# The first cross attention of a two-layer decoder, rewritten as a stage that projects its own keys and values

## The reference, cut to what matters

```
q = x @ Wcq + bcq                 # (4, 256, 128), 16 heads of 8
k = ctx @ Wck + bck               # (4, 1601, 128)
v = ctx @ Wcv + bcv
a = softmax(q k^T / sqrt(8))      # per batch and head: 256 x 1601
o = a v                           # then added, through Wp, to x
```

## Time and profile before

| | |
|---|---|
| three runs | 2718.17, 2724.49, 2734.19 us |
| the profiled execution | 2717.35 us |
| its span | 2715.6 us |
| mean granted TensorE clock | 0.847 of full speed |
| PE busy | 2050.7 us (76%) |
| DVE busy | 1267.7 us (47%) |
| ACT busy | 955.5 us (35%) |
| POOL busy | 389.2 us (14%) |

### The profile page before, as it was taken

How to read it: one execution, slowest core, us unless ns; L and a number is a source line. 1 busy time by engine, 2 the same in 40 slices (tenths; PEclk the granted TensorE clock), 3 DMA queues, 4 the chain that set the end, 5 groups by cost and what they waited for, 6 DMA issues and landing times. The chain is left out here.

```text
span 2715.6 us, 46818 instructions
## 1 busy us (share of the span) xinstructions
PE 2050.7 (76%) x17125; PEld 1118.7 (41%) x17125; DVE 1267.7 (47%) x2794; ACT 955.5 (35%) x1300; POOL 389.2 (14%) x334
## 2 busy tenths in 40 slices
PE   2853396989886299677999336743999999999498
PEld 1532261323334155424666203431455555555365
DVE  2842387778882333351443324534444444442322
ACT  1521161656663222102332113412244444444133
POOL 2110211000000000091111123410111111110100
PEclk7975596888998599797999667976699999999699
DMA  5428723132220001123221165301111111110010
GB/s 175 106 72 226 214 61 75 49 74 66 67 61 1 24 35 35 55 101 112 58 58 39 53 187 135 91 24 46 42 35 36 44 44 44 44 41 2 1 41 29
DMA packets 266743, 183.18 MB, mean 67 GB/s; under 512 B 27924, under 2 KB 252380, under 8 KB 265948
## 3 DMA queue, kind: packets, MB, share of 16 engines
q1 hardware_dynamic: 266588, 181.05, 24.3%
HBM read 92.20 MB, written 65.94 MB: 58 GB/s over the span
## 5 line engine op out<-in xcount | busy, mean ns | idle before, releaser
L1370 DVE TENSOR_REDUCE ta_mxp<-ps 128x1 f32<-128x401 f32 x512 | 267.1, 570 | 314.5 <-PE ps L1295 314.4
L784 DVE TENSOR_REDUCE ac_mxp<-ps 128x1 f32<-128x401 f32 x512 | 273.1, 567 | 44.6 <-PE ps L631 38.0
L1392 ACT ACTIVATE ta_prob<-ps 128x2048 f32<-128x2048 f32 (+1 forms) x112 | 196.6, 1755 | 147.3 <-PE ps L1331 147.3
L856 ACT ACTIVATE ac_prob<-ps 128x1024 f32<-128x1024 f32 (+1 forms) x208 | 210.2, 1024 | 106.0 <-PE ps L667 104.1
L631 PE MATMUL ps<-ac_kb,ac_qz 50*128 50x401 bf16 x512 | 181.9, 383 | 38.1 <-DVE ac_mxp L784 17.1
L784 DVE TENSOR_REDUCE a_mx<-ps 128x4 f32<-128x512 f32 (+1 forms) x160 | 106.9, 670 | 183.3 <-PE ps L635 153.0
L635 PE MATMUL ps<-a_kb,a_qb 64*128 64x256 f32 (+2 forms) x512 | 115.8, 336 | 57.7 <-DMA a_kb<-k 56.8
L1295 PE MATMUL ps<-ta_kb,ta_qb 96*128 96x401 bf16 x512 | 138.5, 354 | 17.9 <-DMA ta_kb<-ta_kh 12.1
L699 PE MATMUL ps<-ac_prob,ac_vs 128*32 128x256 f32 (+1 forms) x1664 | 147.1, 427 | 4.2 <-ACT ac_prob L856 4.2
L1327 PE MATMUL ps<-qxf,ta_k 32*128 32x256 f32 (+1 forms) x1664 | 133.6, 405 | 10.7 <-ACT ta_shiftT L1410 9.2
L1347 PE MATMUL ps<-ta_prob,ta_vs 128*32 128x256 f32 (+1 forms) x1664 | 131.5, 388 | 0.0
(11 more groups left out here) (290 smaller groups left out, 3411.6 us busy)
## 6 DMA issues: line engine op xcount, KB each, us to landing
ta_kb<-ta_kh SPq DMA_DIRECT2D x128, 100.1 KB, 2.2
vc<-c_vt SPq DMA_DIRECT2D x48, 256.0 KB
ac_vs<-vc SPq DMA_DIRECT2D x16, 768.0 KB
a_vs<-v SPq DMA_DIRECT2D x64, 128.0 KB
ac_kb<-kc SPq DMA_DIRECT2D x32, 200.1 KB, 3.5
ta_kb<-ta_kl SPq DMA_DIRECT2D x64, 100.1 KB, 2.2
ta_qb<-a1q SPq DMA_DIRECT2D x32, 192.0 KB, 2.9
ta_kb<-a1k SPq DMA_DIRECT2D x32, 192.0 KB, 3.7
```

The costliest lines, as they stand in the source:

```text
L784: v.tensor_reduce(o, i, AX.X, ALU.max).then_inc(scores_read.s, 1)
L856: a.activation(prob[0:rows, ring, 0:n], banks[0:rows, 0:n], ACT.Exp, scale=scale).then_inc(exp_done.s, 1)
L1370: v.tensor_reduce(mxp[:, qt * G + g, c:c + 1], k.ps[:, turns.bank(slot), 0:401], AX.X, ALU.max).then_inc(scores_read.s, 1)
L1392: a.activation(prob[0:rows, n % 2, :, 0:w], k.ps[0:rows, 2:6, 0:w], ACT.Exp, scale=scale).then_inc(exp_done.s, 1)
```

## The change

- `stage_context` "c0" and the scratch `vc` are gone. "a1" now comes before the load of the context, and the load brings half as much: batches 0 and 1 in partitions 0 to 63, batches 2 and 3 in 64 to 127.
- "ac" is the new `stage_cross8`, written out for all 16 groups. It projects keys once a batch, four slots ("key"), which ACT copies to `k32`; POOL splits them in three parts (`three_parts`), and SP stores them in `kc` and loads each group from there, as before. It projects values once a group in one slot of 13 tiles ("value"), which ACT copies into `vs`; POOL adds their bias.
- All slots (maxima, key, value, sum, shift) share a ring of three banks (0, 1, 7), in the order of `Turns8`.
- A step is two key tiles, so a group has seven steps. The maxima of group s + 1 stand beside steps 1 to 5 of group s, 6 or 7 in a step, none beside steps 0 and 6 (`MAX_AT8`). They run one group ahead, not two.
- Exponents are written to four buffers instead of two, and tiles are weighed one step late.
- The spread denominators ("sum") are inverted by ACT as exp(-log), no longer copied and inverted by DVE.

```diff
+class Turns8:
+    def __init__(self, groups):
+        self.slots = {}
+        self.max_at, self.made_at, self.index = {}, {}, {}
+        self.reads = []
+        for s in range(-1, groups):
+            for p in range(7):
+                m = [("max", s + 1, n) for n in range(*MAX_AT8[p])] if s + 1 < groups else []
+                late = []
+                if s < 0 and p == 0:
+                    late += [("key", 0, c) for c in range(4)]
+                if s >= 0 and s % 4 == 0 and s + 4 < groups and p < 4:
+                    late.append(("key", s // 4 + 1, p))
+                if s + 1 < groups and p == 1:
+                    late.append(("value", s + 1, 0))
+                if s > 0 and p == 2:
+                    late.append(("sum", s - 1, 0))
+                if s + 1 < groups and p == 6:
+                    late.append(("shift", s + 1, 0))
+                self.put((s, p, 0), m[0:3])
+                self.put((s, p, 1), late + m[3:] if s >= 0 or p else late)
+        self.put((groups, 0, 1), [("sum", groups - 1, 0)])
...
+        return (0, 1, 7)[self.index[slot] % 3]
...
+MAX_AT8 = ((0, 0), (0, 6), (6, 13), (13, 19), (19, 26), (26, 32), (32, 32))
+CHUNKS8 = ((0, 401), (401, 400), (801, 400), (1201, 400))
+def stage_cross8(nc, k, name, scale, ctxT, wk, wv, kbias, vbias, qs, ks, out):
...
+                def load(s):
+                    buf = s % 3
+                    if s % 4 == 0:
+                        sp.wait_ge(wrote.s, wrote.at(16 * ks.stores * (s // 4 + 1)))
+                    if s > 2:
+                        sp.wait_ge(st_ready.s, st_ready.at(KT_CTX * (s - 2)))
+                    qs.load_pairs(sp, ops[buf], qz[:, buf, :, :], s, G, LOW)
+                    ks.load_pairs(sp, ops[buf], kb[:, buf, :, :], s, G, LOW)
+                    qs.load_pairs(sp, ops[buf], qb[:, buf, :, :], s, G, LOW)
+                def store(b):
+                    sp.wait_ge(split.s, split.at(4 * (b + 1)))
+                    ks.store(sp, wrote, b * P, kparts[:, :, :], 0, T_CTX)
+                store(0)
+                load(0)
+                load(1)
+                for b in range(B):
+                    load(4 * b + 2)
+                    load(4 * b + 3)
+                    if b + 1 < B:
+                        store(b + 1)
+                        load(4 * b + 4)
+                        load(4 * b + 5)
...
+                def ring(slot):
+                    kind, s, n = slot
+                    free(slot)
+                    bank = k.ps[:, turns.bank(slot), :]
+                    if kind == "max":
...
+                    elif kind == "key":
+                        rows, c0 = context_of(s)
+                        t0, w = CHUNKS8[n]
+                        pe.matmul(bank[:, 0:w], wk[rows, :], ctxT[rows, c0 + t0:c0 + t0 + w],
+                                  start=True, stop=True).then_inc(made.s, 1)
+                    elif kind == "value":
+                        rows, c0 = context_of(s // 4)
+                        for t in range(KT_CTX):
+                            n_ = tile_rows(t)
+                            ins = pe.matmul(bank[0:n_, t * 32:t * 32 + 32], ctxT[rows, c0 + t * P:c0 + t * P + n_],
+                                            wv[rows, s % 4 * 32:s % 4 * 32 + 32], start=True, stop=True)
+                        ins.then_inc(made.s, 1)
+                    elif kind == "sum":
+                        pe.wait_ge(out_read.s, out_read.at(s + 1))
+                        pe.matmul(bank[:, 0:N], k.spread[:, :], sums[:, s % 2, :], start=True, stop=True).then_inc(made.s, 1)
+                    else:
+                        pe.wait_ge(negmax.s, negmax.at(s + 1))
...
+                def transposed_scores(s, t):
+                    if t == 0:
+                        pe.wait_ge(taken.s, taken.at(turns.made_at["shift", s, 0] + 1))
+                    e = s * KT_CTX + t
+                    pe.wait_ge(exp_done.s, exp_done.at(e if t == 0 else max(0, e - 1) if t > 1 else max(0, e - 2)))
...
+                def weigh(s, p):
+                    if p == 0:
+                        pe.wait_ge(biased.s, biased.at(s + 1))
+                        pe.wait_ge(out_read.s, out_read.at(s))
+                    for t in tiles_of(p):
+                        e = s * KT_CTX + t
+                        pe.wait_ge(exp_done.s, exp_done.at(e + 1))
...
+                pe.wait_ge(filled.s, filled.at(3))
+                pe.wait_ge(vfilled.s, vfilled.at(2))
+                for s in range(-1, NS):
+                    for p in range(7):
+                        ts = tiles_of(p)
+                        if s >= 0:
+                            transposed_scores(s, ts[0])
+                        for slot in turns.slots[s, p, 0]:
+                            ring(slot)
+                        if s >= 0 and len(ts) > 1:
+                            transposed_scores(s, ts[1])
+                        if s * 7 + p > 0:
+                            weigh(*divmod(s * 7 + p - 1, 7))
+                        for slot in turns.slots[s, p, 1]:
+                            ring(slot)
+                weigh(NS - 1, 6)
+                ring(("sum", NS - 1, 0))
...
+                v.memset(kflat[LOW:LOW + 2, :].bitcast(F32), ONES).then_inc(vfilled.s, 1)
+                v.memset(vs[:, :, :, :, :], 1.0).then_inc(vfilled.s, 1)
...
+                def exponent(s, t):
+                    e = s * KT_CTX + t
+                    a.wait_ge(st_ready.s, st_ready.at(e + 1))
+                    if e > 3:
+                        s0, t0 = divmod(e - 4, KT_CTX)
+                        a.wait_ge(probs_used.s, probs_used.at(s0 * 7 + t0 // 2 + 1))
...
+                    if kind == "sum":
+                        a.wait_ge(taken.s, taken.at(turns.made_at[slot] + 1))
+                        a.activation(inv[:, s % 2, :], logs[:, :], ACT.Exp, scale=-1.0).then_inc(inverted.s, 1)
...
+                for s in range(-1, NS):
+                    for p in range(7):
+                        if s >= 0:
+                            for t in tiles_of(p):
+                                exponent(s, t)
+                        if s > 0 and p == 0:
+                            results(s - 1)
+                        for slot in turns.slots[s, p, 1]:
+                            if slot[0] != "max":
+                                take(slot)
+                results(NS - 1)
+                take(("sum", NS - 1, 0))
...
+                def three_parts(b):
+                    g_.wait_ge(taken.s, taken.at(turns.made_at["key", b, 3] + 1))
+                    if b > 0:
+                        g_.wait_ge(wrote.s, wrote.at(16 * ks.stores * b))
+                    g_.tensor_copy(kparts[:, 0, :], k32[:, :]).then_inc(split.s, 1)
+                    g_.wait_ge(split.s, split.at(4 * b + 1))
+                    g_.tensor_tensor(krest[:, :], k32[:, :], kparts[:, 0, :], ALU.subtract).then_inc(split.s, 1)
+                    g_.wait_ge(split.s, split.at(4 * b + 2))
+                    g_.tensor_copy(kparts[:, 1, :], krest[:, :]).then_inc(split.s, 1)
+                    g_.wait_ge(split.s, split.at(4 * b + 3))
+                    g_.tensor_tensor(kparts[:, 2, :], krest[:, :], kparts[:, 1, :], ALU.subtract).then_inc(split.s, 1)
...
+                three_parts(0)
+                for s in range(-1, NS):
+                    if s + 1 < NS:
+                        add_bias(s + 1)
+                    if s > 0:
+                        divide(s - 1)
+                    if s >= 0 and s % 4 == 0 and s + 4 < NS:
+                        three_parts(s // 4 + 1)
+                divide(NS - 1)
...
-                v1, vc = Values(nc, "v1", 8, N), Values(nc, "vc", 8, T_CTX)
+                v1 = Values(nc, "v1", 8, N)
...
+                stage_attention(nc, k, "a1", N, 8 ** -0.5, "causal", q1, k1, v1, o1)
                 with ExitStack() as c3:
-                    cT0 = sb_in(c3, "cT0", [P, B * T_CTX])
-                    stage_load(nc, k, [(cT0[0:CC, :], d["ctxT"]), (cT0[CC:P, :], d["ctxT"])])
-                    stage_context(nc, k, "c0", sub(wc0, WC0, "ck"), sub(wc0, WC0, "cv"), col("xck"),
-                                  row("xcv"), kc, vc, cT0, T_CTX)
-                stage_attention(nc, k, "a1", N, 8 ** -0.5, "causal", q1, k1, v1, o1)
-                stage_attention(nc, k, "ac", T_CTX, 8 ** -0.5, None, qc, kc, vc, oc)
+                    cT0 = sb_in(c3, "cT0", [P, 2 * T_CTX])
+                    both = d["ctxT"].rearrange("c (h t) -> c h t", h=2)
+                    stage_load(nc, k, [(cT0[0:CC, :], both[:, 0, :]), (cT0[CC:P, :], both[:, 1, :])])
+                    stage_cross8(nc, k, "ac", 8 ** -0.5, cT0, sub(wc0, WC0, "ck"), sub(wc0, WC0, "cv"), col("xck"),
+                                 row("xcv"), qc, kc, oc)
```

163 lines of the change are left out of this document (added).

## The result

| | before | after |
|---|---|---|
| median, us | 2725.66 (2718.17 to 2734.19, 4 runs) | 2823.49 (2821.71 to 2826.68, 4 runs) |
| span of the profiled execution, us | 2715.6 | 2819.9 |
| stage "ac", us | 421.9 | 619.9 |
| one group of "ac", us | 23.8 | 35.5 |
| granted clock inside "ac" (450:840, 400:900) | 0.87 | 0.62 |

The ratio is 1.0359, with a 95% interval of 1.0327 to 1.0391. The forecast was no change (2723 us, 2688 to 2752). "ac" begins 93.4 us earlier (422.27 before, 328.92 now) and takes 198.0 us more. That makes 104.6, and the spans differ by 104.3: nothing else matters.

The account below looks back on a forecast made before the run. DMAs were taken to bound the context stage and DVE nearly "ac". Start 70.3 + 15 x 27.9 + key slots 9 + last group 18.4 = 516.2 us, 94.3 lost against 95.2 gained: 2723 us, no change, range 2688 to 2752.

Parts of the forecast that it names:

- Removed: Context stage gone, its load kept at half the bytes: 105.9 less 10.7 gives 95.2 us gained.
- New start: Start of "ac" to its first exponent: 70.3 us against 52.3 before, with store and loads in series.
- Border: Between groups: DVE reads the next group's first maximum 4.65 us after the last, waiting for shift, scores and exponent.
- Value slot: Step 1 of a group: weighing and 13 value tiles leave DVE idle 3.5 us before its fourth read.
- Clock behind the value slot: PE at half clock from near the border until about 9 us: 1.8 us more a group, 27.9 in all.
- rival 2: Clock low until the value slot ends: group 29.2 us, kernel 2742 us; chance 0.24.
- The 6 us of the earlier trace: Old "ac": PE at 0.50 for 6 us behind a group's border, the basis for 1.8 us a group.
- Rival 1: PE keeps full clock, dense from step 1 on: group 26.1 us, kernel 2696 us; chance 0.33.
- The Trainium skill: Cited rule for PE: pausing inside its loop, it is throttled again every turn and pays the warm-up each time.
- Key slots: Groups 0, 4 and 8: four more slots of 0.86 us, 3 us each group, 9 us together.
- Rival 3: Three-bank ring fails to speed reads, still 0.52 to 0.53 us apart: group 1.2 us longer, 2741 us; chance 0.07.
- late steps: Steps 3, 4 and 5: scores and weighing between third and fourth maximum leave DVE idle 0.4 us each, 1.2 together.

Follow-up runs that it names:

- even_late_again: m_even with the value slot moved from step 1 to step 4 (ahead of group 0 it stays), a repeat of a slow run; 2751.1 us.
- v_batch_pre3: v_batch with the maxima spread as in m_even, the first three ahead of a group's first transposed scores; 2716.6 us.
- best1_fill: v_batch_pre3 with POOL's key split a group later, and 10 repeated maxima ahead of each border's first transposed scores, 5 behind; 2779.4 us.
- border_fill: Changed kernel plus, in 11 groups, 10 repeated maxima ahead of the first transposed scores and 8 ahead of the first weighing; 2797.8 us.
- the two edits: Against the changed kernel: border_fill, 2797.8 us, and a kernel projecting only one value tile of 13 from the second group on, 2752.8 us.
- v_batch: Changed kernel with values projected once a batch, 128 moving columns a pass instead of 32, in slots of 4, 4, 4 and 1 tiles; 2757.6 us.
- m_even: Changed kernel with the next group's 32 maxima spread over steps 0 to 5 as 6, 6, 5, 5, 5, 5; 2779.0 us.

## Why the prediction was wrong, point by point

- **What bounds it**: right that a group can only be shorter if DVE is kept fed. It wasn't: 323.9 us idle.
- **Removed**: 95.2 forecast, 93.4 measured; the load 10.7 and 10.6.
- **New start**: 70.3 forecast, 64.7 measured; the store was 4.4 us too dear.
- **Border**: DVE reads again after 4.65 us, forecast; in the group above it did so after 0.6 of folding and 4.33 of idle time, 4.9.
- **Value slot**: 3.5 us of idle time, 5.3 with the half clock; measured 6.60. A slot at half clock was priced at 5.8 and takes 5.1 for 23 of 26 loads. At full clock (even_late_again) it is 3.15. The sizes were right, the clock was wrong.
- **Clock behind the value slot**: this is the step that failed. The forecast had "If the clock comes back at 9 us" and gave the half clock 1.8 us a group; even rival 2, at 29.2 us, let it end behind the slot and the sum. In the group above it stayed low to the next border. So the sum slot cost 3.05 in place of 0.8, and three steps 1.9 each in place of 0.4. At full clock the steps do cost 0.48 each (v_batch_pre3 and best1_fill). The excess is (6.60 - 5.3) + (3.05 - 0.8) + (5.68 - 1.2), with 0.3 for the border and 0.3 for the reads 8.6 us, and this group took 36.5 - 27.9 = 8.6 more than forecast. It is a long one. In the group of the windows from 724 us, 34.1 us long, the clock was back 18.5 us after the last read instead of 9 and fell once more; there DVE's idle time is 7.09 us at the value slot, 2.79 at the sum and 1.26, 1.90 and 0.48 in the three steps.
- **The 6 us of the earlier trace rows**: the row fits the kernel before, but not the new group. There PE has maxima of the next group at once and DVE reads on (2.98 of the second 3 us); the new group has none in step 0, and then the value slot. Rival 1 had "dense from step 1 on" as a point for it, without asking dense in what. Its other point, that "ta" is full throughout, is true from 1944 us on only; from 1900 to 1940 "ta" is at 0.50.
- **The Trainium skill**, "TensorE: Matmul & The Clock Gate", HAM oscillation, lays a throttled clock to pauses inside a loop. The trace agrees for the border (border_fill, 26 us). By that rule alone the clock would come back once PE works without pauses, and here it stayed at 0.50 for 23 us with PE busy for 22.4 of them.
- **Key slots**: 3 us a group forecast, 40.5 - 34.7 = 5.8 measured. **Last group and tail**: 18.4, exact.
- **Sum**: 64.7 + 15 x 35.8 + 18.4 = 620, where 516.2 was forecast. The groups are 109 us of the miss, the start gives 5.6 back. The lower end of the range holds a slip: 2696 less 4.3 for the store and less half of the late steps' 1.2 us in 15 groups is 2683, not 2688. It changes nothing here.
- **Rival 3**, the ring: three reads in a row take 1.54 us, 0.487 apart. It does what it should, and it doesn't matter at half clock.

How much of the lost clock is the border's and how much the slot's can't be split cleanly: 26 and 71 us by the two edits, the second with the slot's own time. What in PE's work lets the clock return, and what drops it where neither slot nor border stands (741 us), was not settled. The maxima were never run two groups ahead, as before, so how much of the border is due to that is open too. That the two-tile step as such is too thin was not tried against a step of one tile.

## What to carry to other kernels

Where PE is near to being the bound, price a new stage at both clocks, in every step and not only behind the pause: a group was worth 25.0 or 31.2 us with the same work. Thin float32 slots (26 passes of 32 columns) are worth merging into few wide ones (128 columns, once a batch): v_batch gained 66 us. Useful work moved into the empty step at the border gained 44.5 (m_even). A filler most likely has to stand in the pause itself: behind it, in best1_fill, it only cost.

## What was not expected of the hardware

- PE stayed at 0.50 for 23 us while it was busy for 22.4 of them, and with its maxima doubled a group was no longer than before (35.0 us, 35.5).
- Filling a pause with useless matmuls gave 26 us in border_fill and cost 76 in best1_fill. In the first they followed the shift without a wait, in the second they came behind a pause of 1.01 us; the kernels differ in more than that, so the reason is likely and not shown.
- A DVE instruction of 8 columns took 2.89 us beside a pass of POOL, 17 times its 0.17, while DVE's reductions beside POOL's passes kept their 0.57. The Trainium skill, "SBUF — State Buffer", Who interferes with whom, has it so: a tensor_scalar can take the ports that the two engines share and is then blocked for the whole of the other's instruction, a tensor_reduce never is. The trace agrees in both.
